# Expert outputs written out by token: row scatters in each round in place of 48 row gathers at the end

## What is computed

```
xn = layernorm(x)
x  = x + attention(xn) + experts64(xn)      # layer 0
xn = layernorm(x)
x  = x + rwkv(xn) + experts8(xn)            # layer 1
```

```
top_l, top_i = top_k(xf @ gate_w + gate_b, 3);  gates = softmax(top_l)
pos   = rank of (token, k) within its expert;   valid = pos < 64
buf[e, pos] = xf[token]                          # 64 x 64 slots of 128
y     = gelu(buf @ w1 + b1) @ w2 + b2
out[token] += y[e, min(pos, 63)] * gate * valid  # over k = 0, 1, 2
```

## Time and profile before

| | us |
|---|---|
| three runs | 523.05, 523.83, 525.02 |
| median | 523.83 |
| profiled execution, span from first to last instruction | 525.1 |
| PE busy in it | 494.3 (94%) |
| ACT busy | 375.1 (71%) |
| DVE busy | 303.1 (58%) |
| POOL busy | 144.1 (27%) |

### The profile page before, as it was taken

One profiled execution on the slowest core, in us unless ns is written; L12 is line 12 of the kernel. 1 busy time (PEld: TensorE's weight loads), 2 busy tenths in 40 slices (PEclk: granted clock), 3 DMA queues, 4 the chain that ended last, 5 costly groups with the idle time before them and its releaser, 6 DMA issues.

```text
span 525.1 us, 11527 instructions
## 1 busy us (share of the span) xinstructions
PE 494.3 (94%) x4696; PEld 270.8 (52%) x4696; DVE 303.1 (58%) x790; ACT 375.1 (71%) x464; POOL 144.1 (27%) x133
## 2 busy tenths in 40 slices
PE   6977999999999999999998999999899999999996
PEld 5874223443455455445444232333467766767775
DVE  6799899434343343343330126367937983994895
ACT  3967988786978878978888989888535625553641
POOL 4078000303203203203000445425550755400120
PEclk8997999999999999999998999999899999999999
DMA  5200000565487877977362511100100110000000
GB/s 148 82 1 1 2 1 2 157 216 181 163 238 243 282 243 218 313 238 233 126 201 60 152 32 31 32 1 21 37 6 0 35 38 11 22 0 1 21 1 20
DMA packets 38542, 50.01 MB, mean 95 GB/s; under 512 B 3581, under 2 KB 20250, under 8 KB 38490
## 3 DMA queue, kind: packets, MB, share of 16 engines
q1 hardware_dynamic: 35524, 43.84, 25.4%
q0 software_dynamic: 2560, 5.25, 5.1%
q10 hardware_dynamic: 406, 0.20, 0.1%
HBM read 45.07 MB, written 4.19 MB: 94 GB/s over the span
## 4 chain that ended last, share of the span: by engine, by line
PE 50%; ACT 17%; DVE 6%; issue 5%; DVEq 0%
ACT region_b L564 11%; PE bank L1361 11%; PE scores L1609 9%; PE bank L1618 9%; PE scores L1347 5%; PE bank L1407 4%; PE bank L1395 3%; ACT xn L570 2%; PE bank L1417 2%; PE bank L1478 2%; DVE region_a L1067 2%; ACT L564 2%; ACT L570 2%; DVE base L1078 1%; PE bank L1372 1%
## 5 line engine op out<-in xcount | busy, mean ns | idle before, releaser
L564 ACT ACTIVATE region_b<-scores 128x1024 f32<-128x1024 f32 x256 | 242.4, 1045 | 51.8 <-PE scores L1347 51.6
L1361 PE MATMUL bank<-region_b 128*16 128x256 f32 x2048 | 149.0, 391 | 0.0
L1347 PE MATMUL scores<-region_b 32*128 32x512 f16 x512 | 83.0, 389 | 14.2 <-ACT region_b L564 14.0
L626 ACT ACTIVATE region_b<-scores,small_cols 128x512 f32<-128x512 f32 x64 | 43.6, 685 | 50.3 <-PE scores L1609 50.3
L388 POOL DMA_INDIRECT region_a<-xn_rows,slot_token x32 | 32.5, 1016 | 160.8 <-DVE h_rows L908 108.0
L1361 PEld LDWEIGHTS bank<-region_b 128*16 128x16 f32 x2048 | 42.0, 96 | 57.9 <-issue 42.6
L1618 PEld LDWEIGHTS bank<-region_a,region_b 128*128 128x128 f32 x512 | 62.2, 192 | 15.5 <-issue 15.3
L1347 PEld LDWEIGHTS scores<-region_b 32*128 32x128 f16 x512 | 20.8, 91 | 92.4 <-ACT region_b L564 68.9
L1618 PE MATMUL bank<-region_a,region_b 128*128 128x128 f32 x512 | 62.5, 275 | 0.0
L1609 PE MATMUL scores<-x_rows,region_a 128*128 128x512 f32 x128 | 62.3, 610 | 0.0
L1078 DVE SCALAR_TENSOR_TENSOR base<-bank,g,base 128x128 f32<-128x128 f32 x128 | 36.0, 344 | 28.0 <-PE bank L1618 27.6
(11 more groups left out here) (243 smaller groups left out, 590.6 us busy)
## 6 DMA issues: line engine op xcount, KB each, us to landing
region_a<-in_L_ffn_w SPq DMA_DIRECT2D x64, 512.0 KB, 5.3
region_a<-in_L_ffn_b SPq DMA_DIRECT2D x17, 128.0 KB, 7.2
slot_out<-slots_io SPq DMA_DIRECT2D x8, 256.0 KB, 7.7
region_a<-in_L_attn_x SPq DMA_DIRECT2D x4, 256.0 KB, 4.5
xn_rows<-xn SPq DMA_DIRECT2D x1, 1024.0 KB, 5.1
region_a<-in_L_ffn_W SPq DMA_DIRECT2D x1, 1024.0 KB, 5.9
out<-base SPq DMA_DIRECT2D x4, 256.0 KB, 2.3
region_a<-xn_rows,slot_token POOLq DMA_INDIRECT x32, 3.7
```

The source lines that it names most:

```text
L564: a.activation(PR[:, n % PBUF, 2 * h:2 * h + 2, :], S[:, 2 * h:2 * h + 2, :], ACT.Exp, scale=SCALE).then_inc(s["exp_done"], 1)
L626: a.activation(HS[:, e % 2, k], ps[2 * (e % 2) + k][:], ACT.Relu, bias=COL[:, HC1 * e + k:HC1 * e + k + 1]).then_inc(s["relu_done"], 1)
L1347: last = mm(S[:, j], KT[head, hg, keys], QT[head, hg, BLK * c:BLK * c + BLK], start=True, stop=True)
L1361: last = mm(AV[32 * j:32 * j + VW, cols], VA[:, tile, HG * (g % NHG) + j, :], PR[:, st % PBUF, j, cols], start=(st == 0 and half == 0), st ...
```

## The change

The rounds' outputs are written to a new DRAM tensor `token_out` with a row for each (token, rank), by four indirect scatters a round on POOL, and SP loads whole chunks from it. For that, the slot inversion also gives each slot's rank: `WHO` gets a second half and `invert` has 64 columns, not 32. Slots that hold no pair go to spare rows; rows that no slot writes must be zero, so SP fills 6144 rows (3 MB) at the start. The tile numbers of all steps stay. POOL's order after the rounds becomes `mix(0)`, `mix(1)`, `combine(2)`, `combine(3)`, `mix(2)`, `mix(3)`.

```diff
-    slot_out = nc.dram_tensor("slot_out", [SLOTS, D], F32, kind="Internal").ap()
+    token_out = nc.dram_tensor("token_out", [TOPK * T + P, D], F32, kind="Internal").ap()
...
-        WHO = carve(RA, 6144, 1536, F16).rearrange("p (k t e) -> p k t e", k=TOPK, e=E0)
+        WHO = carve(RA, 6144, 3072, F16).rearrange("p (k t v e) -> p k t v e", k=TOPK, v=2, e=E0)
...
@@ SP, after the store of xn and the load of WG @@
+            sp.wait_ge(s["zero_ready"], 1)
+            sp.dma_start(token_out[0:TOPK * T].rearrange("(p a r) d -> p a (r d)", p=P, r=CH),
+                         OH[:, NC - 1].rearrange("p t g w -> p (t g w)").unsqueeze(1).to_broadcast([P, TOPK * T // (P * CH), BLK])
+                         ).then_inc(s["zeroed"], 16)
             sp.dma_start(MB2[:], mb2_d).then_inc(s["l1_in"], 16)
@@ SP, rounds and after @@
                     sp.wait_ge(s["y_sb"], G)
-                    sp.dma_start(slot_out[P * RING * (G - 1):P * RING * G].rearrange("(i p) d -> p i d", p=P), Y).then_inc(s["y_out"], 16)
                     load_shifts(G)
             sp.wait_ge(s["y_sb"], ROUNDS)
-            sp.dma_start(slot_out[P * RING * (ROUNDS - 1):P * RING * ROUNDS].rearrange("(i p) d -> p i d", p=P), Y).then_inc(s["y_out"], 16)
+            def load_rows(c):
+                rows = token_out[TOPK * BLK * c:TOPK * BLK * (c + 1)].rearrange("(t p k) d -> p t (k d)", p=P, k=TOPK)
+                sp.dma_start(YGS[c % 2].rearrange("p t k d -> p t (k d)"), rows).then_inc(gathered[c], 16)
+            sp.wait_ge(s["y_out"], 16 * RING * ROUNDS)
+            for c in range(EARLY):
+                load_rows(c)
             sp.dma_start(MW1, mw1_d.rearrange("e p h -> p e h")).then_inc(s["mw_in"], 16)
             sp.dma_start(MW2, mw2_d.rearrange("e (c p) d -> p e c d", p=P)).then_inc(s["mw_in"], 16)
+            for c in range(EARLY, NC):
+                sp.wait_ge(s["first_combined"], c - 1)
+                load_rows(c)
@@ POOL @@
+            g.memset(OH[:, NC - 1], 0.0).then_inc(s["zero_ready"], 1)
...
+            def rows_in(G):
+                if G:
+                    pool.wait_ge(s["h_sb"], RING * G)
+                for i in range(RING):
+                    m = RING * G + i
+                    g.indirect_dma_start(ring_in[i], None, xn_rows, bass.IndirectOffsetOnAxis(IDX[:, m:m + 1], 0),
+                                         bounds_check=T - 1, oob_is_err=True).then_inc(ring_in_x[i], 16)
+            def rows_out(G):
+                pool.wait_ge(s["y_sb"], G + 1)
+                for i in range(RING):
+                    m = RING * G + i
+                    if m:
+                        pool.wait_ge(s["y_out"], 16 * m)
+                    g.indirect_dma_start(token_out, bass.IndirectOffsetOnAxis(ROW[:, m:m + 1], 0), Y[:, i, :], None,
+                                         bounds_check=TOPK * T + P - 1, oob_is_err=True).then_inc(s["y_out"], 16)
+            rows_in(0)
+            rows_in(1)
+            pool.wait_ge(s["zeroed"], 16)
+            for G in range(2, ROUNDS):
+                rows_in(G)
+                rows_out(G - 2)
+            rows_out(ROUNDS - 2)
+            rows_out(ROUNDS - 1)
...
-            gather(0)
-            pool.wait_ge(gathered[0], 16 * TOPK * CH)
-            gather(1)
             mix(0)
-            pool.wait_ge(s["first_combined"], 1)
-            gather(2)
+            mix(1)
             combine(2)
-            mix(1)
-            pool.wait_ge(s["first_combined"], 2)
-            gather(3)
             combine(3)
@@ DVE @@
-                link(v.tensor_scalar(VAL[:], POS[:], float(CAP), None, ALU.is_lt))
-                link(v.tensor_scalar(SLF[:], POS[:], float(CAP - 1), None, ALU.min))
-                ix = IXF[:].rearrange("p t k -> p k t")
-                link(v.scalar_tensor_tensor(SLF[:], ix, float(CAP), SLF[:], ALU.mult, ALU.add))
-                v.tensor_copy(SLG[:], SLF[:]).then_inc(s["ranked"], 1)
+                v.tensor_scalar(VAL[:], POS[:], float(CAP), None, ALU.is_lt).then_inc(s["ranked"], 1)
...
-                    v.tensor_tensor(WHO[:, k], EQ[:, k], TOK[:].unsqueeze(2).to_broadcast([P, NT, E0]), ALU.mult)
+                    v.tensor_tensor(WHO[:, k, :, 0, :], EQ[:, k], TOK[:].unsqueeze(2).to_broadcast([P, NT, E0]), ALU.mult)
+                    v.tensor_scalar(WHO[:, k, :, 1, :], EQ[:, k], float(k + 1), None, ALU.mult)
...
-                v.tensor_copy(IDX[:], ps[6][:, 0:NPAIR]).then_inc(s["slot_ready"], 1)
+                v.tensor_copy(IDX[:], ps[6][:, 0:NPAIR])
+                link(v.tensor_copy(RNK[:, 0], ps[6][:, NPAIR:2 * NPAIR]))
+                link(v.tensor_scalar(RNK[:, 1], RNK[:, 0], 0.5, SPARE[:], ALU.is_lt, ALU.mult))
+                link(v.tensor_tensor(RNK[:, 1], RNK[:, 1], RNK[:, 0], ALU.add))
+                link(v.tensor_scalar(RNK[:, 1], RNK[:, 1], -1.0, None, ALU.add))
+                v.scalar_tensor_tensor(ROW[:], ps[6][:, 0:NPAIR], float(TOPK), RNK[:, 1], ALU.mult, ALU.add).then_inc(s["slot_ready"], 1)
...
-                    dve.wait_ge(s["y_out"], 16 * G)
+                    dve.wait_ge(s["y_out"], 16 * RING * G)
...
-                dve.wait_ge(gathered[c], 16 * TOPK * CH)
+                dve.wait_ge(gathered[c], 16)
@@ PE, invert @@
-                            last = mm(ps[6][CAP * odd:CAP * odd + CAP, 0:NPAIR], RANK[:, k, t, :], WHO[:, k, t, odd:E0:2],
+                            last = mm(ps[6][CAP * odd:CAP * odd + CAP, 0:2 * NPAIR], RANK[:, k, t, :], WHO[:, k, t, :, odd:E0:2],
```

More of the change, by code:

```diff
@@ L176, in build @@
         VAL = sb("valid", [P, TOPK, NT])
-        SLF = sb("slot_f", [P, TOPK, NT])
-        SLG = sb("slot_gather", [P, TOPK, NT], U32)
         TOK = sb("token", [P, NT])
         IDX = sb("slot_token", [P, NPAIR], U32)
+        SPARE = sb("spare_row", [P, 1])
+        RNK = sb("slot_rank", [P, 2, NPAIR])
+        ROW = sb("slot_row", [P, NPAIR], U32)
         MH = sb("mask_bf", [P, NT, E0], BF16)
@@ L234, in build @@
             qk_ready exp_done av_done a_evac ep_ps ep_used top_ready gexp_ready mask_ready count_ready slots_ready
-            ranked inverted slot_ready b1_in b1_ps b1_sb b2_in bt_ps bt_sb up_done h_sb gelu_done htr_ps htr_sb down_done y_sb
+            ranked inverted slot_ready zero_ready zeroed b1_in b1_ps b1_sb b2_in bt_ps bt_sb up_done h_sb gelu_done htr_ps htr_sb down_done y_sb
             ot_ps ot_sb x1_ps x1_sb var2_ready std2_ready xn2_ready xn2t_ps xn2t_sb lg2_ps l8_ready p8_exp g_ready
@@ L346, in _ @@
                             pattern=[[1, P]], channel_multiplier=-1)
+            g.iota(SPARE[:], [[0, 1]], base=TOPK * T + 1, channel_multiplier=1, allow_small_or_imprecise_dtypes=True)
             g.iota(iota_e[:], [[1, E0]], base=0, channel_multiplier=0, allow_small_or_imprecise_dtypes=True)
@@ L384, in _ @@
             pool.wait_ge(s["late_split"], 2 * (NC - EARLY))
-            for m in range(NPAIR):
-                if m >= RING and m % RING == 0:
-                    pool.wait_ge(s["h_sb"], m)
-                g.indirect_dma_start(ring_in[m % RING], None, xn_rows, bass.IndirectOffsetOnAxis(IDX[:, m:m + 1], 0),
-                                     bounds_check=T - 1, oob_is_err=True).then_inc(ring_in_x[m % RING], 16)
-            pool.wait_ge(s["y_out"], 16 * ROUNDS)
-            def gather(c):
-                for t in range(CH * c, CH * c + CH):
-                    if t > CH * c:
-                        pool.wait_ge(gathered[c], 16 * TOPK * (t - CH * c))
-                    for k in range(TOPK):
-                        g.indirect_dma_start(YGS[c % 2][:, t - CH * c, k, :], None, slot_out, bass.IndirectOffsetOnAxis(SLG[:, k, t:t + 1], 0),
-                                             bounds_check=SLOTS - 1, oob_is_err=True).then_inc(gathered[c], 16)
+            def rows_in(G):
[21 more added lines that the diff above has]
+            rows_out(ROUNDS - 1)
             def combine(c):
-                pool.wait_ge(gathered[c], 16 * TOPK * CH)
+                pool.wait_ge(gathered[c], 16)
                 chunk = slice(CH * c, CH * c + CH)
```

## The result

| | before | after |
|---|---|---|
| median of 4 runs each, us | 523.44 (521.29 to 525.02) | 554.99 (554.78 to 555.83) |
| profiled execution, span, us | 525.1 | 553.0 |
| first to last `moe_y` of the eight rounds, us | 137.8 | 160.3 |

A forecast was written before the change was run, and what follows sets the result against it. PE held half the chain that ended last, and removing the gathers was worth at most 0.4 us. Added costs 5.2 + 3.0 + 1.4 = 9.6 on a median of 523.8 gave 533.4 us, range 530 to 536 (wider range 527 to 541).

The forecast's parts named there:

- Parts 1 and 2: Chunk 2: DVE waits for combine(2) behind mix(1), 5.2 us; combine(3)'s adds then hold up DVE, 3.0, its multiply nothing.
- Part 3: Slot inversion: 64 columns in place of 32 lengthen PE's 96 matmuls by 1.4 us; bounds 0 and 1.7.
- Parts 4 and 5: Before the rounds: DVE's added work ahead of the inversion and SP's zero fill, landing within 15.3 us, each cost 0.
- Part 6: The rounds: four serial scatters at 4.2 us a step fit DVE's 19.1 and POOL's 19.8 us; cost 0.
- (a): The rounds, first rival: scatters don't fit; at a step of 4.9, 9 us more, 542.4; chance 0.20.
- (b): Chunk 2: no exclusion between DVE and POOL, or DVE keeps its turn; 4.3 us, so 528.1; chance 0.10.
- (c): The start: the zero fill is slow, 3.5 us more, 536.9; chance 0.03.
- (d): Chunk 2: combine(2) stays hidden and combine(3) does no harm, so only the inversion counts; 525.2; chance 0.07.
- (e): PE's clock: one half-speed stretch more or fewer, some 1 to 2 us either way; only widens the range, no chance given.
- DVE idle at `x1_norm(2)`: Sign in chunk 2: DVE's L945 idle some 5 us for POOL's add.
- L1082 to L1086: Sign in chunk 1's mix: these DVE operations, L1058 to L1062 before the change, take over 1.5 us.
- ACT's 3 us: Sign after the slot inversion: ACT idle near 3 us, not 1.58.

The follow-up runs named there:

- Run 5: run 2 with combine(2) and combine(3) put back to where DVE waits for PE: 522.6 us, ratio 0.997.
- run 4: The changed kernel without the weight loads of rounds 1 to 7, scatters still waiting for one another: 532.7 us, ratio 1.018.
- run 2: The changed kernel with a DRAM tensor and semaphore for each of a round's four scatters, only the first tensor loaded back: 529.1 us, ratio 1.012.
- Run 10: The changed kernel with two sets of token tiles, two output tiles and the two combines where DVE waits for PE: 524.4 us, ratio 1.002.

## Why the prediction was wrong

**Parts 1 and 2 (5.2 + 3.0) were right.** Both kernels' rows are 21.65 us apart at L1075, the first scan (410.38, now 432.03). DVE starts `x1_norm(2)` at 441.28 where 414.84 + 21.65 = 436.49 would have been: 4.8 late, with the scan held to 3.70 by POOL's multiply. At the end of `time_mix_out(1)` it is 7.2 late, so `combine(3)` adds 2.4 for the 3.0. PE's `finish(1)` is 8.1 late; the missing 0.9 is PE's own: after its wait its clock was granted at 0.57 in 450 to 454 and 0.50 in 454 to 456. Run 5 takes the two combines away from there and saves 8.0. The Trainium skill's rule ("SBUF — State Buffer", Who interferes with whom) is borne out: L1077 and L1082 to L1084, which stretched, have two SBUF inputs, while L1102, with one input from PSUM, kept its 1.13 us beside POOL. One stretch is not of that kind: L978, with one SBUF input, took 0.56 us for 0.17, until POOL's multiply was done, so Part 2's "costs nothing" for the multiply is 0.4 short. (The 24 gathers in the earlier trace rows are those of chunks 0 and 2, not the first 24; nothing hangs on it, as DVE's two combines waited 0.4 us in all.)

**Part 3 (1.4) was zero.** The inversion with twice the columns, and ACT's wait after it, in the changed kernel:

```profile
94.05 1.71 PE L1464 MATMUL bank<-region_a 128*64 128x64 f16 x96
...
96.12 1.02 ACT L586 ACTIVATE region_b<-scores 128x1024 f32<-128x1024 f32 x1 [1.60 <-PE scores L1371]
```

1.71 against 1.70, 1.60 against 1.58. The line between 32 and 128 columns was the wrong interpolation: the pitch is the same at 32 and 64, so the lower bound, 0, holds. That the weight load sets it, the reason given for that bound, is not shown.

**Parts 4 and 5 (0) were right.** PE came to the inversion with the same 0.4 us of idle time as before. The fill landed in 12.6 us, under the 15.3 of the bound, and nothing waited for it.

**Part 6 (0) is the step that failed.** It said "4.2 a step" and "Both fit, POOL by 0.6. It fails from a step of 4.4." In rounds 0 to 6 there are 21 waits: 88.6 less the last round's 6.1 is 82.5, or 3.9 each, and with the issue a step of 4.9. The 4.2 took its 3.7 of landing from the fetches of before. The scatters go out at another time: right behind `moe_y`, which is when SP issues the next four weight loads of 512 KB. SP's queue in the changed kernel, where the first two `moe_y` start at 147.36 and 168.72:

```profile
147.35 2.08 SPq L291 DMA_DIRECT2D region_a<-in_L_ffn_w  x4
...
167.16 1.91 SPq L291 DMA_DIRECT2D region_a<-in_L_ffn_w  x4
```

The first step of that round is its longest, 7.1. That the weights do it is shown by run 4, which takes them away; by which way they do it, HBM, the DMA engines or the order of their queues, no run shows. The page of before had a row nearer to the scatters than the fetches are: SP's store of the same tile at the same moment, though behind the weights on SP's own queue (KB each, median us to landing).

```profile
slot_out<-slots_io SPq DMA_DIRECT2D x8, 256.0 KB, 7.7
```

The size alone doesn't explain 22.5 us. At 4.9 the prediction's own first rival gives 9. Its formula compares a mean step with a mean round, as if POOL's queue could run late in one round and catch up in the next. With one output tile and one set of token tiles it can't: run 2, in which no scatter waits, shows when the fetch is free to go, and when PE takes it:

```profile
159.49 1.05 POOL L410 DMA_INDIRECT region_a<-xn_rows,slot_token  x1 [7.74 <-DVE h_rows L933]
...
170.46 0.60 PE L1409 MATMUL bank<-ident,region_a 128*128 128x128 f32 x4
```

That is 14.2 and 25.1 us after the round's `moe_y` at 145.32. With steps of 4.2 and the first scatter 1.5 after `moe_y`, the fetch would go at 1.5 + 3 x 4.2 + 1.3 = 15.4, 1.2 late; its fourth issue is 4.0 on, and with 3.7 of landing it is home at 23.1: inside. In the change it goes at 167.68, 20.3 after `moe_y`. It is also slow to land, 7.3 us in the middle of its four against 3.0 for the same fetch of before, and it now goes out just behind the next weight loads, those of 167.16. So PE stops. Round by round against before, the seven gaps between `moe_y`s grew by 1.6 (DVE's wait), 7.4 (a fetch), 7.2 (DVE's wait), 1.1, 0, 6.6 (a fetch) and, once, shrank by 1.3. A stop costs more than its length: PE waited 5.7 and 4.9 us for the two fetches, and the gaps grew by 1.7 more each. After these stops its clock was granted at 0.50 (in 179 to 183 after the first), and the same work took nearly twice as long. PE's timeline of the changed kernel after the first stop:

```profile
180.53 1.91 PE L1385 MATMUL bank<-region_b 128*16 128x256 f32 x16
...
184.60 1.06 PE L1385 MATMUL bank<-region_b 128*16 128x256 f32 x16
```

The 1.1 behind DVE's second wait is of the same kind (0.50 in 222 to 228). By these differences some 4.5 of the 22.5 us are PE at half speed.

The formula counted the time that POOL takes to issue the fetches behind the scatters, but not the moment by which PE needs them, and not that one tile and one set leave no slack to average over. Run 10 gives a round of slack, and in its trace the same chain, at 24.3 us a round, costs PE next to nothing.

**The rivals.** (a) is what happened, at its step of 4.9 but two and a half times its price. (b) falls by the 3.70 of L1077. (c) falls by the 12.6. (d) falls by the 2.72 of L969. (e) came both ways: half-speed stretches of before are gone and others stand behind the stops. Of the signs, DVE idle at `x1_norm(2)` came with 2.72 rather than 5 because the scan before it had taken up the rest, PE's 5.63 at L1497 came as said, of L1082 to L1086 only two took over 1.5 us, and ACT's 3 us did not come; "the forecast is wrong if L924 waits for the scatters" is what the profile of after shows at L948.

## What to carry over

A chain of dependent DMAs on an in-order queue is priced by the landing at the moment when it goes out, not by the median of other DMAs, and by the due time of whatever stands behind it on the same queue. Mean against mean only holds where buffers give slack to average over: with one tile a single late round counts and is not made up for, PE's half speed behind each stop comes on top, and mending one of two waits that come from one late queue only moves the loss to the other. When slow transfers go, ask what they held in place: here 24 gathers had kept two POOL combines in the gaps of DVE, and 8 of the 31.6 us are the price of letting them run as soon as POOL came to them.

## What the runs showed of the hardware

An indirect write to HBM with idle DMAs takes a step of 3.0 us (wait 2.04), less than the 3.31 of an indirect read into SBUF, which waits for a group of three. The rule that the prediction cited against the change, that the receipt of the last write is longest where the target is HBM (the Trainium skill, "DMA: Bandwidth & Descriptors", Anatomy of one DMA — SWDGE path), is therefore not seen in these rows as a longer step; what made the step longer was the weight loads, 3.5 at the longest wait without them and 7.8 with. PE's pitch for a matmul with 64-column weights was 17.8 ns with 64 moving columns and 17.7 with 32. After a stop of some 5 us in the rounds, PE's granted clock was 0.50 for the next 3 to 5 us.
